# A transformer block on one core: the next token tile is loaded one unit ahead in SyncE's list, and GpSimd issues four of sixteen strip transfers

## The chip, the core and the metric

The kernel runs on one core of a Trainium2 chip. Five engines with an instruction list each work side by side: TensorE (PE in the profile; PEld is its weight load), VectorE (DVE), ScalarE (ACT), GpSimd (POOL) and SyncE (SP), which only issues transfers. They wait for each other through semaphores. The metric is the time of one execution in microseconds (us), median of several.

## The reference

For `x` of 8 x 1024 tokens x 256: `xn = layernorm(x)`, and the output is `x + attention(xn) + ffn(xn)`.

```
qkv = einsum('bse,ehd->bshd', xn, w_qkv);  q, k, v = split(qkv, 3)      # 16 heads of 64
probs = softmax(where(causal, q.k / sqrt(64), neg))
attention = einsum('bshd,hde->bse', einsum('bhqk,bkhd->bqhd', probs, v), w_out)

scores = softmax(xn @ wg); top 2 of 8 experts, their scores made to sum to 1
ffn = sum over the two chosen experts of gate * (relu(row @ w1[e] + b1[e]) @ w2[e] + b2[e])
      # at most 2048 rows an expert; rows beyond that are dropped
```

## The kernel before, in words

Three stages: layernorm, router and routing (up to about 100 us), the eight experts (to about 900 us), and attention with the final sum (from about 910 us to the end). The change lies in the last one, `attention_and_sum`.

**Units and steps.** Attention runs in 64 units: 8 batch entries x 8 pairs of heads. A unit `n` has 20 steps. Each engine has its own list, written out by loops over `(n, s)`, and an engine works its list strictly in order. Rows of the score matrix (tiles of 128 queries, `i` = 0 to 7) are treated in five rounds (steps 0, 4, 8, 12, 16): rows 3 and 2, rows 4 and 1, rows 5 and 0, row 6, row 7. For a round TensorE makes the scores `S` (L1230); VectorE masks them, takes the row minimum of their negative and writes `pr` (L1353); ScalarE exponentiates and sums (L1291); VectorE inverts the sums (`rinv`, L1359); GpSimd scales `pr` by them (L1433).

**Turning the probabilities.** The product with the values needs them transposed (`pT`). Rows 0 to 3 are transposed by TensorE (L1186) and copied by ScalarE (L1281). Rows 4 to 7 are transposed in 32x32 squares by VectorE (L1395, tile `squares`), and then sixteen SBUF-to-SBUF transfers a group put the squares in place: `place(n, 2)` for rows 4 and 5 (96 KB each), `place(n, 3)` for rows 6 and 7 (128 KB each), both L1084. `place(n, 2)` is issued late in unit n (it waits for the squares of row 5, step 14); `place(n - 1, 3)` is issued in unit n, since row 7 of unit n - 1 is squared at step 2 of unit n. TensorE multiplies by the values (L1261, tile `O`) for unit n - 1 in three runs: at step 3 of unit n (rows 0 to 3), at step 7 (rows 4, 5) and at step 15 (rows 6, 7). ScalarE and VectorE split the result into two parts (`oh` L1322, `ol` L1402), TensorE multiplies by `w_out` (L1175, pieces `o0` to `o3`), and VectorE adds to `res` (L1379).

**The next batch entry.** Queries, keys and values are products of the layernorm output `xn`, held transposed. While a batch entry is worked on, the tiles of the next one are brought in, one a unit: SP loads a tile of 128 tokens into `xnt` (L1102), TensorE transposes it at step 1 (piece `xn`, L1164), ScalarE and VectorE split it (L1297, L1369). Nine tiles are there at the start (`AHEAD`), so units 0 to 54 have this piece and units 55 to 63 do not. There is one buffer `xnt`: its next load waits until the transposes of the tile before are done.

**SyncE's list in a unit** is: load `xnt`; load the weights of unit n + 2 (L1072, waits for GpSimd's split of those of n + 1, L1445); `place(n - 1, 3)`; `place(n, 2)`; in even units, the value weights (L1076). Once in eight units it also stores `res` (L1088) and refills it (L1093). A wait at the head of this list holds all that is behind it.

**GpSimd's list in a unit**: scale round 4 of the unit before; split weights (L1438, L1442, L1445); scale round 0 (step 4); `total` (step 5: adds the expert output to one tile of `res`, L1490); `choose` (L1460); scale round 1 (step 8); two gathers `fetch0` and `fetch1` of expert rows (L1468); scale round 2 (step 12); `weigh` and `add` (L1474, L1479); scale round 3. In unit n, `total` adds to tile (n - 1) mod 8 of `res`, and VectorE's addition `o{g}` in unit n waits for it where that tile lies in group g. So `o0`, at VectorE's step 6, waits for GpSimd's `total` in units with n mod 8 of 1 or 2.

Of the kernel before, what the change touches and what calls it, by code (L numbers as in the profile page):

```python
# [19 lines left out]
TILES = TOKENS // P  # L20
# [469 lines left out]
class Start:  # L490


    TILES = QT + 1
# [352 lines left out]
def attention_and_sum(nc, k, x, xn_dram, w_qkv, w_out, pick, y_dram, out, start):  # L846
# [8 lines left out]
    AHEAD = Start.TILES  # L855
    VW = 4 * HDIM
    BL = 32
    QUARTERS = P // BL
# [50 lines left out]
    RUN_OF = {g: j for j, groups in enumerate(RUN_GROUPS) for g in groups}  # L909
# [6 lines left out]
                return n - later, j  # L916
        return None

    POOL_AT = {"split_w": 1, "total": 5, "choose": 6, "fetch0": 8, "fetch1": 9, "weigh": 13, "add": 14, "split_wv": 17}

    turns_of = lambda i: [t for t in TURNS if i in [at[0] for at in TURNS[t]]]
    turn_unit = lambda n, t: n if t in STEP_OF else END_STEP[TURNS[t][0][0]][0]
# [21 lines left out]
    with ExitStack() as c:  # L944
        sb = lambda n, s, d=F32: c.enter_context(nc.sbuf_tensor(n, s, d))
        ps = lambda n, s: c.enter_context(nc.psum_tensor(n, s, F32))
        sem = lambda n: c.enter_context(nc.semaphore(n))
# [16 lines left out]
        xnt = sb("xnt", [P, MODEL])  # L964
# [14 lines left out]
        xnv = xn_dram.rearrange("(t p) m -> t p m", p=P)  # L979
# [51 lines left out]
        score, negmax, expd, scaled = (Count(sem(f"s_{n}"), len(ORDER)) for n in ("score", "negmax", "expd", "scaled"))  # L1031
        recip = Count(sem("s_recip"), len(ROUNDS))
        squared = Count(sem("s_squared"), 2 * len(SQUARED))
        placed = {g: Count(sem(f"s_placed{g}"), 16 * QUARTERS * QUARTERS) for g in (2, 3)}
        pv = Count(sem("s_pv"), RUNS)
        ohi, olo = Count(sem("s_ohi"), RUNS), Count(sem("s_olo"), RUNS)
        filled = Pieces(sem("s_filled"), lambda name: True)
# [25 lines left out]
        def strip(g, a, b):  # L1063

            to, of = slice(b * BL, (b + 1) * BL), slice(a * BL, (a + 1) * BL)
            return wide[g][to, a].rearrange("p x r -> p (x r)"), sq[g][of, b].rearrange("p x k i -> p (x k i)")

        @block.sync
        def _(e):
            def load_w(m):  # L1070
                for c_ in range(MC):
                    e.dma_start(wr[:, 2 * c_:2 * c_ + 2], wv[m % PAIRS][:, c_, :, 0:2 * HDIM]).then_inc(wload.sem, 16)  # L1072

            def load_wv(m):
                for c_ in range(MC):
                    e.dma_start(wvr[:, c_], wvv[m % (PAIRS // 2)][:, c_, :, 2 * HDIM:]).then_inc(wvload.sem, 16)  # L1076

            def place(n, g):
                e.wait_ge(squared.sem, squared.at(n, 4 * g - 4))
                if n > 0:  # L1080
                    e.wait_ge(pv.sem, pv.at(n - 1, RUN_OF[g] + 1))
                for a in range(QUARTERS):
                    for b in range(QUARTERS):
                        e.dma_start(*strip(g, a, b)).then_inc(placed[g].sem, 16)  # L1084

            def store(b, g):
                e.wait_ge(dve.sem, dve.at((b + 1) * PAIRS, f"o{g}"))
                e.dma_start(outv[:, b, 2 * g:2 * g + 2], res[:, 2 * g:2 * g + 2]).then_inc(stored[g].sem, 16)  # L1088

            def refill(b, g):  # L1090
                if b > 0:
                    e.wait_ge(stored[g].sem, stored[g].at(b - 1, 16))
                e.dma_start(res[:, 2 * g:2 * g + 2], xv[:, b, 2 * g:2 * g + 2]).then_inc(rload[g].sem, 16)  # L1093

            load_w(1)
            load_wv(1)
            for n in range(UNITS):
                b, u = n // PAIRS, n % PAIRS
                if n + AHEAD < TILES:
                    if n > 0:  # L1100
                        e.wait_ge(filled.sem, filled.at(n - 1, "xn"))
                    e.dma_start(xnt[:], xnv[n + AHEAD]).then_inc(xload.sem, 16)  # L1102
                if n == 0:
                    e.wait_ge(s_wolo, 1)
                    for g in range(GROUPS):
                        refill(0, g)
                if n + 2 < UNITS:
                    e.wait_ge(wlo.sem, wlo.at(n, MC))
                    load_w(n + 2)
                if n > 0:  # L1110
                    place(n - 1, 3)
                if b > 0 and u == 0:
                    for g in range(3):
                        store(b - 1, g)
                    for g in range(3):
                        refill(b, g)
                if n < UNITS - 1:
                    place(n, 2)
                if n % 2 == 0 and n // 2 + 2 < UNITS // 2:
                    e.wait_ge(wvlo.sem, wvlo.at(n // 2, MC))  # L1120
                    load_wv(n // 2 + 2)
                if b > 0 and u == 0:
                    store(b - 1, 3)
                    refill(b, 3)
            for g in range(GROUPS):
                store(BATCH - 1, g)
            for g in range(GROUPS):
                e.wait_ge(stored[g].sem, stored[g].at(BATCH - 1, 16))

        @block.tensor  # L1130
        def _(e):
# [103 lines left out]
            def values(n, j):  # L1235
                groups = RUN_GROUPS[j]
                if in_squares(n, 2 * groups[0]):
                    g = groups[0]
                    e.wait_ge(placed[g].sem, placed[g].at(n + 1, 0))
                else:  # L1240
                    for m, name in [(turn_unit(n, t), t) for g in groups for i in (2 * g, 2 * g + 1) for t in turns_of(i)]:
                        if by_act(name):
                            e.wait_ge(act.sem, act.at(m, name))
                        else:
                            e.wait_ge(dve.sem, dve.at(m, name))
                if j == 0:
                    e.wait_ge(act.sem, act.at(n // 2 * 2 - 1, "v1"))
                    if n > 0:
                        e.wait_ge(olo.sem, olo.at(n - 1, RUNS))
                else:  # L1250
                    e.wait_ge(act.sem, act.at(n // 2 * 2, "v1"))
                    e.wait_ge(olo.sem, olo.at(n, j))
                for g in groups:
                    KT, o0 = 2 * g + 2, g % 2 * GQ
                    for kt in range(KT):
                        a = P if kt == KT - 1 else 0
                        for h in range(2):
                            hs = slice(h * HDIM, (h + 1) * HDIM)
                            vs = slice(n % 2 * P + h * HDIM, n % 2 * P + (h + 1) * HDIM)
                            turned_p = wide_of(g, h, kt, a // P) if in_squares(n, 2 * g) else pT[g][:, h, kt, a:GQ]  # L1260
                            ins = e.matmul(O[hs, o0 + a:o0 + GQ], vv[n // 2 % 2][:, kt, vs], turned_p,  # L1261
                                           start=(kt == 0), stop=(kt == KT - 1))
                ins.then_inc(pv.sem, 1)
# [73 lines left out]
        def _(e):  # L1337
# [52 lines left out]
            def square(n, i, h):  # L1390
                g, KT = i // 2, i + 1
                if n > 0 and i % 2 == 0 and h == 0:
                    e.wait_ge(placed[g].sem, placed[g].at(n, 0))
                e.wait_ge(scaled.sem, scaled.at(n, SCALE_ORDER.index((i, h)) + 1))
                e.transpose(sq[g][:, :, 2 * h + i % 2, 0:KT, :],  # L1395
                            room_of(n, i, h)[:, OFFSET[i]:OFFSET[i] + KT * P].rearrange("p (k b i) -> p b k i", b=QUARTERS, i=BL)
                            ).then_inc(squared.sem, 1)
# [30 lines left out]
        def _(e):  # L1428
# [18 lines left out]
            def split_wv(m):  # L1447
# [6 lines left out]
                for c_ in range(MC):  # L1454
                    e.tensor_tensor(wvl[:, c_], flat(wvr[:, c_]), wvh[:, c_].bitcast(F32), ALU.subtract).then_inc(wvlo.sem, 1)

            def choose(m):
                if m > 0:
                    e.wait_ge(summed.sem, summed.at(m - 1, 1))
                e.tensor_copy(sel[:], pick[:, m, :]).then_inc(picked.sem, 1)  # L1460
# [33 lines left out]
            for n, s in ALL + END:  # L1494
                r, x = s // SUB, s % SUB
                m, q = back(n, s, SUB)[0], (r - 1) % len(ROUNDS)
                if x == 0 and 0 <= m < UNITS:
                    for j in range(FIRST[q], FIRST[q + 1]):
                        scale(m, j)
                for name, at in POOL_AT.items():  # L1500
                    if s != at:
                        continue
                    if name == "total" and n > 0:
                        total(n - 1)
                    if n == UNITS:
                        continue
                    if name == "choose":
                        choose(n)
                    elif name == "split_w" and n + 1 < UNITS:
                        split_w(n)  # L1510
                    elif name == "split_wv" and n % 2 == 0 and n // 2 + 1 < UNITS // 2:
                        split_wv(n // 2)
                    elif name[:5] == "fetch":
                        fetch(n, int(name[5]))
                    elif name == "weigh":
                        weigh(n)
                    elif name == "add":
                        add(n)
# [38 lines left out]
```

## Time and profile before

| | |
|---|---|
| median of 3 runs | 3215.53 us (3213.91 to 3217.07) |
| profiled execution, its own time | 3221.27 us |
| its span | 3219.3 us |
| PE busy | 2905.2 us, 90% |
| DVE, ACT, POOL busy | 65%, 53%, 46% |
| mean granted TensorE clock | 0.946 of full speed |

Busy shares are averages over three stages with different limits, so each stage has to be looked at alone. "Idle before" a group of instructions is the time in which their engine had nothing running right before them, and the arrow names what ended it. SPq is SyncE's list of transfers: its times are those of the issues, not of the movement of data. A row of several instructions (xN) has the start of the first, and the time to the end of the last for those that touch.

### The profile page before, as it was taken

The page shows a single profiled execution, that of the slowest core. Times are in us where ns is not written, and L with a number is a line of the kernel's source. Part 1 is how long each engine was busy: PE and PEld are TensorE (multiplying, and loading weights), DVE is VectorE, ACT ScalarE, POOL GpSimd, SP SyncE. Part 2 cuts the span into 40 slices and gives each one's busy share as a digit, 9 for nine tenths or more (in the row PEclk, how much of TensorE's full clock was granted, in tenths as well). Part 3 has the DMA queues.
Part 4 walks back from the last instruction along what each step waited for, and adds up shares of the span by engine and source line. Part 5 has one row for each costly group of instructions (what it writes and reads, how often), then busy time and mean ns, then how long its engine had stood idle before and what let it go on. Part 6 is the DMA issues. An engine that isn't in the chain of part 4 may idle for free.

```text
span 3219.3 us, 61016 instructions
## 1 busy us (share of the span) xinstructions
PE 2905.2 (90%) x21321; PEld 2337.3 (73%) x21321; DVE 2107.3 (65%) x4448; ACT 1714.3 (53%) x3934; POOL 1465.3 (46%) x2127
## 2 busy tenths in 40 slices
PE   4699999999989988999899898989889998999998
PEld 3589998999967666777667676766667766777776
DVE  7744434444357776777777777777767777778785
ACT  3444444454445555555555555555555555556664
POOL 3122222122135555555555555555555555556663
PEclk8799999999999998999899999999989999999999
DMA  7112222122135455546555555555565455555653
GB/s 236 49 47 73 74 72 71 55 67 74 52 99 122 117 128 147 132 116 148 126 133 123 138 129 126 131 142 123 125 152 125 118 123 148 129 128 149 150 126 91
DMA packets 252805, 371.57 MB, mean 115 GB/s; under 512 B 77392, under 2 KB 177744, under 8 KB 252512
## 3 DMA queue, kind: packets, MB, share of 16 engines
q1 hardware_dynamic: 240192, 334.14, 40.9%
q0 software_dynamic: 12320, 33.60, 3.6%
q8 instruction: 174, 2.85, 0.4%
q14 instruction: 119, 0.97, 0.1%
HBM read 102.80 MB, written 33.55 MB: 42 GB/s over the span
## 4 chain that ended last, share of the span: by engine, by line
PE 36%; SPq 15%; DVE 7%; issue 5%; DMA 5%; POOL 3%; ACT 1%; DVEq 0%; POOLq 0%; ACTq 0%
SPq L1084 14%; PE O L1261 13%; PE S L1230 9%; DMA xnt<-xn 4%; PE W L1175 4%; PE W L1186 4%; DVE squares L1395 3%; PE W L1141 3%; PE W L1156 3%; DVE pr L1353 2%; POOL pr L1433 2%; PE W L1164 1%; SPq L1076 1%; ACT pr L1291 1%; DMA out<-res 1%
## 5 line engine op out<-in xcount | busy, mean ns | idle before, releaser
L1433 POOL TENSOR_SCALAR pr<-pr,rinv 128x512 f32<-128x512 f32 (+7 forms) x1024 | 747.8, 746 | 959.8 <-DVE rinv L1359 958.6
L1291 ACT ACTIVATE pr<-pr,negm 128x512 f32<-128x512 f32 (+7 forms) x1024 | 784.4, 771 | 146.4 <-DVE negm L1353 146.2
L1353 DVE CUSTOM_DVE_ANT_0 pr<-S,late 128x512 f32<-128x512 f32 (+7 forms) x1024 | 718.1, 752 | 154.8 <-PE S L1230 154.4
L1261 PE MATMUL O<-pT,vv 128*64 128x256 f32 (+1 forms) x5120 | 631.4, 405 | 1.8 <-DMA pT<-squares 1.1
L1261 PEld LDWEIGHTS O<-pT,vv 128*64 128x64 f32 x5120 | 398.7, 155 | 222.8 <-issue 82.0
L1395 DVE STREAM_TRANSPOSE squares<-pr 128x640 f32<-128x640 f32 x504 | 494.8, 1020 | 0.3 <-POOL pr L1433 0.3
L832 DVE TENSOR_TENSOR hl<-h,hh 128x512 fp32r<-128x512 f32 x256 | 190.6, 745 | 322.0 <-ACT hh L793 311.0
L789 ACT ACTIVATE h<-pH,b1c 128x512 f32<-128x512 f32 x256 | 175.8, 687 | 369.8 <-PE pH L719 342.0
L1281 ACT ACTIVATE pT<-W 128x512 f32<-128x512 f32 (+3 forms) x520 | 200.2, 435 | 321.0 <-PE W L1186 320.3
L731 PE MATMUL pY<-w2h,hh 128*128 128x256 f32 x1024 | 287.8, 281 | 2.5 <-DVE hl L832 2.5
L731 PE MATMUL pY<-w2l,hh 128*128 128x256 f32 x1024 | 289.0, 282 | 0.0
L731 PE MATMUL pY<-w2h,hl 128*128 128x256 f32 x1024 | 287.8, 281 | 0.0
L1402 DVE TENSOR_TENSOR ol<-O,oh 128x256 fp32r<-128x256 f32 (+1 forms) x192 | 98.2, 512 | 235.5 <-ACT oh L1322 235.5
L1230 PE MATMUL S<-khf,qh 64*128 64x512 f32 (+2 forms) x1024 | 220.5, 426 | 1.5 <-DVE negm L1353 1.5
L1141 PE MATMUL W<-xnh,wh 128*128 128x512 f32 x512 | 215.2, 420 | 2.7 <-DVE klf L1387 1.5
L1186 PE MATMUL W<-ident,pr 128*128 128x128 f32 x1332 | 201.8, 282 | 17.0 <-POOL pr L1433 11.9
L1164 PE MATMUL W<-ident,xnt 128*128 128x128 f32 x110 | 31.5, 383 | 204.9 <-DMA xnt<-xn 204.9
L719 PE MATMUL pH<-xh,w1h 128*128 128x512 f32 x512 | 206.4, 403 | 4.6 <-DVE xl L804 2.6
L719 PE MATMUL pH<-xl,w1h 128*128 128x512 f32 x512 | 202.7, 396 | 0.0
L1141 PE MATMUL W<-xnh,wl 128*128 128x512 f32 x512 | 202.7, 396 | 0.0
L719 PE MATMUL pH<-xh,w1l 128*128 128x512 f32 x512 | 202.6, 396 | 0.0
L1141 PE MATMUL W<-xnl,wh 128*128 128x512 f32 x512 | 202.6, 396 | 0.0
(175 smaller groups left out, 6346.5 us busy)
## 6 DMA issues: line engine op xcount, KB each, us to landing
pT<-squares SPq DMA_DIRECT2D x1008, 128.0 KB
pT<-squares SPq DMA_DIRECT2D x1008, 96.0 KB, 2.1
y<-yb SPq DMA_DIRECT2D x128, 128.0 KB, 1.7
wr<-in_L_attn_w_qkv SPq DMA_DIRECT2D x128, 128.0 KB, 2.3
x<-in_L_attn_x SPq DMA_DIRECT2D x16, 512.0 KB, 9.0
xn<-xn SPq DMA_DIRECT2D x16, 512.0 KB, 4.7
w1r<-in_L_ffn_w SPq DMA_DIRECT2D x8, 1024.0 KB
w2r<-in_L_ffn_w SPq DMA_DIRECT2D x8, 1024.0 KB
```

The source lines that it names most:

```text
L719: ins = e.matmul(pH[hc % 4][:], w[par][:, m, ws], xx[q][:, m, :], start=(n == 0), stop=(n == 3 * MC - 1))
L731: ins = e.matmul(pY[t % 2][:], hs[q][:, hc, ts_], ws[par][:, hc, :], start=(hc == 0 and n == 0), stop=(hc == HC - 1 and n == 2))
L1084: e.dma_start(*strip(g, a, b)).then_inc(placed[g].sem, 16)
L1141: ins = e.matmul(W, ws[:, 2 * m + of_k], xs[:, t0:t0 + HT, m, :], start=(i == 0), stop=(i == 3 * MC - 1))
L1186: ins = e.transpose(W[:, at * P:(at + 1) * P], room_of(unit, i, h)[:, cols], k["ident"][:])
L1230: ins = e.matmul(S[h][:, off + f * HALF:off + f * HALF + cols], t[hs, i * P:(i + 1) * P], u[f][n % 2][hs, 0:cols], start=(j == 0), stop=(j ...
L1261: ins = e.matmul(O[hs, o0 + a:o0 + GQ], vv[n // 2 % 2][:, kt, vs], turned_p, start=(kt == 0), stop=(kt == KT - 1))
L1281: ins = e.activation(dst, src, ACT.Copy) if by_act(name) else e.tensor_copy(dst, src)
L1291: e.activation(p, p, ACT.Exp, bias=negm[:, c0:c0 + 1], scale=-1.0, accum_out=rsum[:, c0:c0 + 1]).then_inc(expd.sem, 1)
L1353: e.tensor_tensor_reduce(room_of(n, i, h)[:, off:off + w], S[h][:, off:off + w], late[:, SEQ - w:], 1.0, -MASKED, ALU.add, ALU.min, negm[: ...
L1395: e.transpose(sq[g][:, :, 2 * h + i % 2, 0:KT, :], room_of(n, i, h)[:, OFFSET[i]:OFFSET[i] + KT * P].rearrange("p (k b i) -> p b k i", b=Q ...
L1433: e.tensor_scalar(p, p, rinv[:, c0:c0 + 1], 1.0, ALU.mult, ALU.mult).then_inc(scaled.sem, 1)
```

## The change

In SyncE's list the load of `xnt` stands behind the weight load of the same unit and is that of the next unit's tile; the first one stands ahead of the loop. It waits for the transposes of this unit's tile (`filled.at(n, "xn")`). Of the sixteen transfers of `place(n - 1, 3)`, SyncE issues twelve; GpSimd issues the last four, at its step 4, after the scaling of round 0 and ahead of `total`. They count on a semaphore of their own, `pool_placed`, for which TensorE (before the third run) and VectorE (before it writes the squares of row 6 again) wait as well.

```diff
-    POOL_AT = {"split_w": 1, "total": 5, "choose": 6, "fetch0": 8, ...
+    POOL_AT = {"split_w": 1, "place3": 4, "total": 5, "choose": 6, "fetch0": 8, ...
@@
-        placed = {g: Count(sem(f"s_placed{g}"), 16 * QUARTERS * QUARTERS) for g in (2, 3)}
+        placed = {2: Count(sem("s_placed2"), 16 * QUARTERS * QUARTERS), 3: Count(sem("s_placed3"), 16 * QUARTERS * (QUARTERS - 1))}
+        pool_placed = Count(sem("s_pool_placed"), 16 * QUARTERS)
@@ def place(n, g):
-                for a in range(QUARTERS):
+                for a in range(QUARTERS - (g == 3)):
@@ sync
+            e.dma_start(xnt[:], xnv[AHEAD]).then_inc(xload.sem, 16)
             load_w(1)
             load_wv(1)
             for n in range(UNITS):
                 b, u = n // PAIRS, n % PAIRS
-                if n + AHEAD < TILES:
-                    if n > 0:
-                        e.wait_ge(filled.sem, filled.at(n - 1, "xn"))
-                    e.dma_start(xnt[:], xnv[n + AHEAD]).then_inc(xload.sem, 16)
@@
                 if n + 2 < UNITS:
                     e.wait_ge(wlo.sem, wlo.at(n, MC))
                     load_w(n + 2)
+                if n + 1 + AHEAD < TILES:
+                    e.wait_ge(filled.sem, filled.at(n, "xn"))
+                    e.dma_start(xnt[:], xnv[n + 1 + AHEAD]).then_inc(xload.sem, 16)
                 if n > 0:
                     place(n - 1, 3)
@@ tensor, values(n, j); vector, square(n, i, h) alike
                     e.wait_ge(placed[g].sem, placed[g].at(n + 1, 0))
+                    if g == 3:
+                        e.wait_ge(pool_placed.sem, pool_placed.at(n + 1, 0))
@@ gpsimd
+            def place_rest(n):
+                e.wait_ge(squared.sem, squared.at(n + 1, 0))
+                if n > 0:
+                    e.wait_ge(pv.sem, pv.at(n - 1, RUN_OF[3] + 1))
+                for b in range(QUARTERS):
+                    e.dma_start(*strip(3, QUARTERS - 1, b)).then_inc(pool_placed.sem, 16)
@@
+                    if name == "place3" and n > 0:
+                        place_rest(n - 1)
```

SyncE's list through a unit (2 here; every later one is alike), as it was. `pT<-squares` of 32x1024 is `place(n - 1, 3)`, that of 32x768 is `place(n, 2)`; lines are one higher in the changed kernel:

```order
L1102 DMA xnt<-xn 128x256 [waits s_filled]
L1072 DMA wr<-in_L_attn_w_qkv 128x2x128 [waits s_wlo_a]
L1072 DMA wr<-in_L_attn_w_qkv 128x2x128
L1084 DMA pT<-squares 32x1024 [waits s_pv,s_squared]
L1084 DMA pT<-squares 32x1024 x15
L1084 DMA pT<-squares 32x768 [waits s_pv,s_squared]
L1084 DMA pT<-squares 32x768 x15
```

And the same unit as it stands now:

```order
L1073 DMA wr<-in_L_attn_w_qkv 128x2x128 [waits s_wlo_a]
L1073 DMA wr<-in_L_attn_w_qkv 128x2x128
L1110 DMA xnt<-xn 128x256 [waits s_filled]
L1085 DMA pT<-squares 32x1024 [waits s_pv,s_squared]
L1085 DMA pT<-squares 32x1024 x11
L1085 DMA pT<-squares 32x768 [waits s_pv,s_squared]
L1085 DMA pT<-squares 32x768 x15
```

The load of the tile that a unit transposes has moved from right behind `place(n - 1, 2)` of the unit before to ahead of both placements of the unit before.

GpSimd's list from the end of the weight split to the gathers, as it was:

```order
L1445 TENSOR_TENSOR wl<-wr,wh 128x256
L1433 TENSOR_SCALAR pr<-pr,rinv 128x512 [waits s_recip] x2
L1433 TENSOR_SCALAR pr<-pr,rinv 128x384 [waits s_recip] x2
L1490 TENSOR_TENSOR res<-res,yg 128x256 [waits s_dve,s_sum1]
L1460 COPY sel<-pick 128x4 [waits s_summed]
L1433 TENSOR_SCALAR pr<-pr,rinv 128x640 [waits s_recip] x2
L1433 TENSOR_SCALAR pr<-pr,rinv 128x256 [waits s_recip] x2
L1468 DMA yg<-y,sel 128x256 [waits s_picked] x2
```

And now:

```order
L1450 TENSOR_TENSOR wl<-wr,wh 128x256
L1438 TENSOR_SCALAR pr<-pr,rinv 128x512 [waits s_recip] x2
L1438 TENSOR_SCALAR pr<-pr,rinv 128x384 [waits s_recip] x2
L1467 DMA pT<-squares 32x1024 [waits s_pv,s_squared]
L1467 DMA pT<-squares 32x1024 x3
L1502 TENSOR_TENSOR res<-res,yg 128x256 [waits s_dve,s_sum1]
L1472 COPY sel<-pick 128x4 [waits s_summed]
L1438 TENSOR_SCALAR pr<-pr,rinv 128x640 [waits s_recip] x2
L1438 TENSOR_SCALAR pr<-pr,rinv 128x256 [waits s_recip] x2
L1480 DMA yg<-y,sel 128x256 [waits s_picked] x2
```

The four issues stand between the scaling of round 0 and `total` (the addition to `res`); the scaling of round 1 and all behind it follow them.

## Rows read from the trace of the kernel before

**Rows 1.** Tile `xnt`: durations in ns (min/median/max), idle before it, landing.

```profile
L1164 PE MATMUL W<-ident,xnt x110: 271/421/449, 925.5 to 2879.8; 128*128 128x128 f32 x110
L1102 SPq DMA_DIRECT2D xnt<-xn x55: 467/505/663, 912.5 to 2877.3; - x55
  DMA xnt<-xn: 204.9, 54
DMA to landing us min/median/max: 2.1/2.4/2.9
```

**Rows 2.** SyncE's queue through a unit (start us, us, what, count).

```profile
2007.41 0.89 SPq L1072 DMA_DIRECT2D wr<-in_L_attn_w_qkv  x2
2008.40 30.15 SPq L1084 DMA_DIRECT2D pT<-squares  x32
2038.59 1.19 SPq L1076 DMA_DIRECT2D wvr<-in_L_attn_w_qkv  x2
2039.82 0.50 SPq L1102 DMA_DIRECT2D xnt<-xn  x1
```

**Rows 3.** Stretches: us, busy of each engine, granted clock, DMA share, GB/s.

```profile
962.90:2884.00 1921.10, 1722.24 (x13040) 1321.26 (x13036) 1390.36 (x3021) 1063.07 (x2650) 1050.83 (x1590) 0.93 0.54 130
2889.85:3142.90 253.05, 243.55 (x1954) 189.26 (x1954) 204.74 (x448) 157.90 (x393) 158.99 (x240) 1.00 0.57 143
3004.40:3035.90 31.50, 30.45 (x247) 23.62 (x246) 25.64 (x57) 19.72 (x50) 20.96 (x32) 1.00 0.54 129
```

**Rows 4.** TensorE's timeline at the piece `xn` and the next transposes.

```profile
925.53 0.38 PE L1164 MATMUL W<-ident,xnt 128*128 128x128 f32 x2
958.41 0.66 PE L1164 MATMUL W<-ident,xnt 128*128 128x128 f32 x2 [6.76 <-DMA xnt<-xn]
...
993.27 0.41 PE L1164 MATMUL W<-ident,xnt 128*128 128x128 f32 x2 [2.76 <-DMA xnt<-xn]
...
997.62 1.09 PE L1186 MATMUL W<-ident,pr 128*128 128x128 f32 x8
...
2879.62 0.52 PE L1164 MATMUL W<-ident,xnt 128*128 128x128 f32 x2 [2.51 <-DMA xnt<-xn]
...
2885.52 0.66 PE L1186 MATMUL W<-ident,pr 128*128 128x128 f32 x4
```

**Rows 5.** Waits from 2915 to 3142 us: total, times, longest.

```profile
PE W L1186 <- POOL pr L1433: 8.1, 8, 1.0
PE O L1261 <- DMA pT<-squares: 1.1, 1, 1.1
```

**Rows 6.** Timeline of unit 58: GpSimd.

```profile
3011.58 2.48 POOL L1433 TENSOR_SCALAR pr<-pr,rinv 128x512 f32<-128x512 f32 x4
3014.03 0.73 POOL L1490 TENSOR_TENSOR res<-res,yg 128x256 f32<-128x256 f32 x1
3014.83 0.18 POOL L1460 COPY sel<-pick 128x4 uint32<-128x4 uint32 x1
3017.27 2.49 POOL L1433 TENSOR_SCALAR pr<-pr,rinv 128x640 f32<-128x640 f32 x4 [2.25 <-DVE rinv L1359]
3019.90 1.03 POOL L1468 DMA_INDIRECT yg<-y,sel  x1
3021.24 0.96 POOL L1468 DMA_INDIRECT yg<-y,sel  x1 [0.30 <-issue]
3023.34 2.49 POOL L1433 TENSOR_SCALAR pr<-pr,rinv 128x128 f32<-128x128 f32 x4 [1.14 <-DVE rinv L1359]
```

**Rows 7.** Timeline of unit 58: VectorE and TensorE.

```profile
3014.87 0.69 DVE L1379 TENSOR_TENSOR res<-W,res 128x512 f32<-128x512 f32 x1 [0.64 <-POOL res L1490]
3016.99 0.18 DVE L1359 RECIPROCAL rinv<-rsum 128x4 f32<-128x4 f32 x1 [1.43 <-ACT pr L1291]
3017.42 0.42 DVE L1402 TENSOR_TENSOR ol<-O,oh 128x256 fp32r<-128x256 f32 x1 [0.25 <-ACT oh L1322]
3019.12 0.36 PE L1175 MATMUL W<-woh,oh 128*128 128x256 f32 x1
3021.49 1.56 DVE L1395 STREAM_TRANSPOSE squares<-pr 128x640 f32<-128x640 f32 x2
3027.25 1.83 DVE L1395 STREAM_TRANSPOSE squares<-pr 128x768 f32<-128x768 f32 x2
```

**Rows 8.** GpSimd's and SyncE's issues: ns min/median/max, first and last start.

```profile
L668 POOL DMA_INDIRECT xg<-xn,slot_token x8: 942/946/2535, 136.2 to 147.5; - x8
L1084 SPq DMA_DIRECT2D pT<-squares x2016: 507/592/2192, 944.1 to 3179.7; - x184
```

More of the change, by code:

```diff
@@ L917, in run_at @@
         return None
-    POOL_AT = {"split_w": 1, "total": 5, "choose": 6, "fetch0": 8, "fetch1": 9, "weigh": 13, "add": 14, "split_wv": 17}
+    POOL_AT = {"split_w": 1, "place3": 4, "total": 5, "choose": 6, "fetch0": 8, "fetch1": 9, "weigh": 13, "add": 14, "split_wv": 17}
     turns_of = lambda i: [t for t in TURNS if i in [at[0] for at in TURNS[t]]]
@@ L1393, in square @@
                     e.wait_ge(placed[g].sem, placed[g].at(n, 0))
+                    if g == 3:
+                        e.wait_ge(pool_placed.sem, pool_placed.at(n, 0))
                 e.wait_ge(scaled.sem, scaled.at(n, SCALE_ORDER.index((i, h)) + 1))
@@ L1506, in _ @@
                         continue
-                    if name == "choose":
+                    if name == "place3" and n > 0:
+                        place_rest(n - 1)
+                    elif name == "choose":
                         choose(n)
```

## The prediction

> **What bounds the kernel now.** I read the page's split by slices and then the waits of the attention stage, which is 2300 of 3219 us. TensorE has one large wait there: 204.9 us in 54 places in front of the transposes of `xnt`, ended by that tile's transfer [rows 1]. Nothing else holds TensorE for more than a microsecond or two. SyncE's queue says why the tile is late: its issue (2039.82) stands directly behind a run of 32 strip issues and the value weights [rows 2]. The second half of that run cannot start before row 5 is squared, late in the unit; the tile then lands 2.4 us after its issue [rows 1]. TensorE wants it at step 1 of the next unit, and so a chain goes round once a unit: squares, sixteen issues, load, transposes, scores, squares.
>
> The profile holds its own counter-example. The units from 55 on have no `xnt` load but the same strips, products and softmax. The table of stretches shows both kinds [rows 3]. With the load: a granted clock of 0.93, near but not at the upper of TensorE's two levels (2.4 GHz), and units that take (2879.62 - 958.41) / 53 = 36.25 us [rows 4]. Without it: clock 1.00, TensorE busy 243.55 of 253.05 us, and units of 31.50 us, in which it is busy 30.45 [rows 3]. The loss is thus larger than the wait of 3.7 us. From the transposes of `xnt` to the next ones (L1186) TensorE took 4.35 us at 993.27, but 5.90 us at 2879.62 [rows 4], and most units look like the second: the wait is followed by a stretch at the lower level (1.2 GHz), which costs 1.5 us.
>
> **The load.** It moves ahead of both placements. It now waits for this unit's transposes (step 1), which come before the squares of row 7 (step 2) that the placement behind it wants; so this wait holds nobody, and the tile has nearly a unit to land. The 0.5 us issue in front of twelve strips instead of sixteen still ends them sooner than before. I take the wait as gone, all of it.
>
> What is late next stands in the last units too: TensorE waits 1.0 us for GpSimd's scaling of round 0, in each of 8 units [rows 5], since GpSimd splits weights right before it. A unit with an `xn` piece adds its transposes on TensorE, 0.41 us [rows 4], and one subtraction on VectorE just ahead of the reciprocal for which GpSimd waits, of about the same size. The first fits into the 1.0 us, the second pushes GpSimd by most of its length. I take 0.35 us, hence 31.85 us a unit. (Bounds: 31.5 if all hides, 31.9 if none does: -19 to +3 us over the kernel.)
>
> - 53 intervals of 36.25 - 31.85 = 4.40: 233.2 us.
> - The interval from 925.53 to 958.41 holds a wait of 6.76 us [rows 4]; unit 0 has less work, and I take back 1.0 for the next limit: 5.8 us.
> - The slow stretch behind the last transposes, 5.90 - 4.35: 1.5 us.
> - The wait of 1.1 us for strips [rows 5], in the unit where a store had held SyncE: four strips fewer take at least 4 x 0.51 us [rows 8], so it goes: 1.1 us.
>
> Sum 241.6 us. 3221.3 - 241.6 = 2979.7 us by the profiled execution.
>
> **The four issues on GpSimd.** SyncE gets 4 x 0.59 us a unit back [rows 8], worth nothing now that it has slack. GpSimd pays. The trace has no plain transfer issued by GpSimd, so p, the distance from one issue to the next, is bounded: from below by SyncE's 0.6 us (0.59 median, [rows 8]); from above by the longest gather issue, 2.54 us plus the 0.30 us gap between two [rows 6, 8]: 2.84 us. The nearest row is the pair of gathers: 3019.90 to 3021.24 is 1.34 us, and the shortest gather is 0.94, with the gap 1.24 [rows 6, 8]. I take p = 1.25, since a strip has 32 rows where a gather has 128, but no row shows that rows count.
>
> Three things stand behind them, read in unit 58.
>
> - `total` (3014.03) starts 4p later. In units with n mod 8 of 1 or 2, VectorE's `o0` waits for it: this happens here already (0.64 us, [rows 7]). `o0` would start at 3014.87 + 4p; behind it on VectorE come the reciprocal and `ol`, so `ol` ends 0.69 + 0.18 + 0.42 + 0.1 later, at 3016.3 + 4p. TensorE wants it at 3019.12 for `o1` [rows 7]. TensorE is late by 4p - 2.8, for p = 1.25: 2.2 us. Nothing later in the unit gives it back, as TensorE has no other idle time but the 1.0 us whose chain moves with it. These are 16 units: 35 us. A stop of 1.1 us left the clock at 1.00 in the stretch that holds it [rows 3, 5], while one of 2.51 was followed by the slow level [rows 4]. 2.2 lies between; I charge a third of 1.5 us: 8 us.
> - The scaling of round 1 can start at 3015.1 + 4p instead of 3017.27 and has row 4 ready for the squares (3021.49) by 3016.0 + 4p for its first head [rows 6, 7]: in time up to p = 1.37. Nothing for the other units.
> - The gathers and the scaling of round 2 follow: it would start near 3020.2 + 4p = 3025.2 instead of 3023.34 and have row 5's first head ready 1.6 us later, 3026.8, before VectorE's 3027.25 [rows 6, 7]. Nothing, but only just.
>
> For larger p VectorE falls behind in every unit, by 4p - 5.45 at row 5's squares. It has about 1.95 us of idle time behind them before the last round's reciprocal, on which GpSimd's scaling and then TensorE's transposes hang. A general unit is late by 4p - 7.4, from p = 1.85 on.
>
> **Where a page bears on it.** The two gather issues beside a busy VectorE in unit 58 took 1.03 and 0.96 us [rows 6]. The Trainium skill (SBUF — State Buffer, section "SBUF: two separate sides") says that a transfer issued by GpSimd has its descriptors written by GpSimd's cores, which are locked out of a shared port while VectorE runs an instruction in a two-port mode, and gives 620 ns for such a transfer alone and about 3100 ns beside a VectorE copy. By the first figure the sum would be near the lower bound below, by the second it would be the slower rival. VectorE's work in that stretch is of other kinds (one operand in PSUM), and the trace's gathers side with the short figure.
>
> **The sum.** 2979.7 + 35 + 8 = 3022.7 us for the profiled execution, which is 5.7 us above the median of the runs shown (3221.27 against 3215.53). Expected median: 3017 us.
>
> **The rivals.**
>
> 1. *GpSimd's issues are cheap*, p up to 0.7: 4p - 2.8 is 0, nothing is late. 2979.7 - 5.7 = 2974 us. For it: a strip is simpler than a gather. Against it: no GpSimd issue in the trace is under 0.94 us.
> 2. *They are dear enough to reach every unit*, p = 2: 16 x (5.2 + 1.5) + 48 x 0.6 = 136 us, giving 3110 us. For it: one issue of 2.54 us; four in a row are not shown. Against it: 946 ns is the median of such issues.
> 3. *Slower than before.* The same place, GpSimd's step 4: the loss 16 x (4p - 1.3) + 48 x (4p - 7.4) eats the 241.6 us at p = 2.41. At p = 2.84, the upper bound, it is 161 + 190 = 351 us: 3325 us. It decides at 2.41 us an issue.
> 4. *The clock stays at 0.93* though TensorE waits less: 54 units x 7% of 31.85 are 120 us less gain, some 3137 us. Against it: 1.00 over 253 us of the same work, and 0.93 only beside the waits [rows 3].
> 5. *The load isn't the chain*: its transfer is still late, or the wait turns up at the next strips. Within 0.2% of before, 3215 us. Against it: the last units place the same strips without a wait, but the one of 1.1 us.
>
> **How the numbers follow.** Forecast (p from 1.0 to 1.5) 0.58; rival 1, 0.2; rival 2, 0.12; rival 3, 0.04; rival 4, 0.04; rival 5, 0.02. The range takes in p = 0.7 and, below it, half of the 19 us that a unit of 31.5 would give: 2966. Above, p = 1.65 gives 16 x (3.8 + 1.5) = 85 us, 3059; with a little of rival 2, 3064. Faster by more than 0.2% (about what this kernel's measurement can tell from no change): all but rivals 3 and 5, 0.94; within 0.2%, 0.02; slower, 0.04.
>
> **What would show it.** The wait of TensorE for `xnt` (204.9 us) is gone, and `xnt`'s issue stands some 25 us ahead of its transposes. The granted clock from 963 us on is near 1.00. TensorE waits about 1 us a unit for GpSimd at L1438. The distance of two strip issues on GpSimd is 1.25 us. In 16 units, and only there, VectorE's addition `o0` waits for GpSimd's `total`, 4 to 5 us, and TensorE waits some 2 us for `ol`. I am wrong if units without that wait take much over 31.9 us, if the wait for `xnt` has become one for strips, or if the issues on GpSimd take under 0.7 or over 1.5 us.

## The result: 2980 us, 7.3% faster, near the lower bound of the term on GpSimd

| | before | changed |
|---|---|---|
| median | 3216.3 us (4 runs, 3213.9 to 3218.9) | 2980.22 us (4 runs, 2979.75 to 2982.94) |
| ratio | | 0.9268, 95% interval 0.9252 to 0.9284 |
| span of the profiled execution | 3219.3 us | 2978.6 us |

The forecast was 3017 us, with a range of 2966 to 3064. The direction, the mechanism and the size of the gain from the load came out as forecast; the loss charged to GpSimd's four issues (43 us) did not appear. The nearest case was rival 1, cheap issues, 2974 us.

**The wait for the load.** The changed kernel's answer for tile `xnt` (durations in ns, first and last start):

```profile
L1165 PE MATMUL W<-ident,xnt x110: 270/271/273, 922.9 to 2639.8; 128*128 128x128 f32 x110
L1110 SPq DMA_DIRECT2D xnt<-xn x54: 461/466/535, 928.9 to 2612.9; - x54
```

There is no waiting row under it any more, where [rows 1] has 204.9 us in 54 places. The transposes themselves have gone from a median of 421 ns to 271: they are no longer run right after a stop. The last load is issued at 2612.9 and wanted at 2639.8, 27 us later.

From these rows and [rows 1] the whole gain can be counted. First to last transposes: 1954.3 us before, 1716.9 now, 237.4 us less. What stands ahead of the first ones: 2.6 us less. What stands behind the last ones: 339.5 against 338.8 us. Sum 240.7 us, the difference of the spans.

**The clock.** Stretches of the changed kernel: us, busy of PE, PEld, DVE, ACT, POOL, granted clock, DMA share, GB/s. The first is units with an `xn` piece, the second units without.

```profile
963.00:2640.00 1677.00, 1612.10 (x12916) 1253.34 (x12914) 1360.74 (x2992) 1048.61 (x2626) 1153.28 (x1780) 1.00 0.58 148
2655.00:2900.00 245.00, 236.08 (x1888) 183.02 (x1888) 199.81 (x437) 152.19 (x377) 169.37 (x262) 1.00 0.54 142
```

Against 0.93 in [rows 3] the clock is 1.00, and TensorE is busy 96% of both. Per unit it was busy 1722.24 us / 53.0 = 32.5 us before (1921.10 / 36.25 units) and is now busy 1612.10 / 52.6 = 30.7 us (1677 / 31.9 units) with the same work: 1.8 of the 4.35 us by which a unit got shorter (36.25 to 31.90 on average, without the first) go with the clock.

**What is left.** The waits of the changed kernel from 950 to 2900 us: total, times, longest.

```profile
PEld W L1187 <- DVE xnl L1372: 68.7, 53, 1.3
PE W L1187 <- POOL pr L1438: 68.0, 62, 1.2
DVE res L1382 <- POOL res L1502: 44.2, 16, 3.1
PE O L1264 <- DMA pT<-squares: 5.0, 6, 1.8
```

The second row is the wait of [rows 5], now in every unit. The first is the same stop as TensorE's weight loads show it. The name in it is only that of the last thing that ended before: in the unit at 2102 us `xnl` was over 1.0 us before the load began (2101.97 against 2102.95), so it did not end the wait, though it can delay what did (see e7 below). The third row is the expected one: VectorE waits for GpSimd's `total` in 16 units. TensorE shows no wait behind it.

**GpSimd in such a unit**, to be read beside [rows 6], and below VectorE and TensorE, beside [rows 7]:

```profile
2770.80 2.48 POOL L1438 TENSOR_SCALAR pr<-pr,rinv 128x512 f32<-128x512 f32 x4
2773.22 2.08 POOL L1467 DMA_DIRECT2D pT<-squares  x4
2775.32 0.74 POOL L1502 TENSOR_TENSOR res<-res,yg 128x256 f32<-128x256 f32 x1
2776.13 0.18 POOL L1472 COPY sel<-pick 128x4 uint32<-128x4 uint32 x1
2777.05 2.50 POOL L1438 TENSOR_SCALAR pr<-pr,rinv 128x640 f32<-128x640 f32 x4 [0.73 <-DVE rinv L1362]
2779.70 1.06 POOL L1480 DMA_INDIRECT yg<-y,sel  x1 [0.16 <-issue]
```

All of GpSimd's strip issues (ns, min/median/max):

```profile
L1467 POOL DMA_DIRECT2D pT<-squares x252: 489/512/606, 955.4 to 2932.2; - x126
```

VectorE and TensorE in the same unit:

```profile
2776.17 0.69 DVE L1382 TENSOR_TENSOR res<-W,res 128x512 f32<-128x512 f32 x1 [2.72 <-POOL res L1502]
2776.78 0.17 DVE L1362 RECIPROCAL rinv<-rsum 128x4 f32<-128x4 f32 x1
2778.34 0.36 PE L1176 MATMUL W<-woh,oh 128*128 128x256 f32 x1
```

Four issues take 2.08 us with no gap: p = 0.52 us, less than half of the 1.25 that I took, and below SyncE's 0.59. So a plain strip of 32 rows is much cheaper to issue than a gather of 128, which still takes 1.06 us in the same unit. The scaling of round 1 even waits 0.73 us for its reciprocal. VectorE's `o0` is over (2776.8) 1.5 us before TensorE comes to `o1` (2778.34).

### The profile page after: what moved, and what is told of

It is laid out like the page before. It is cut to its first block, busy times and chain, and to the rows that moved or that the text cites. A ratio compares the mean times of both kernels' runs of the same rounds, so it can differ in the third digit from the quotient of the medians.

```text
span 2978.6 us, 61141 instructions
## 1 busy us (share of the span) xinstructions
PE 2802.8 (94%) x21321; PEld 2276.4 (76%) x21321; DVE 2089.6 (70%) x4448; ACT 1710.1 (57%) x3934; POOL 1601.7 (54%) x2379
## 4 chain that ended last, share of the span: by engine, by line
POOL 24%; PE 23%; issue 17%; ACT 3%; DVE 2%; DMA 0%; POOLq 0%; DVEq 0%; ACTq 0%
POOL pr L1438 14%; PE O L1264 5%; PE S L1231 5%; PE W L1187 4%; PE W L1142 3%; PE W L1176 3%; POOL wl L1450 3%; PE W L1157 2%; ACT pr L1294 2%; POOL wh L1447 2%; POOL wvl L1460 1%; POOL yg L1486 1%; POOL wr L1443 1%; POOL wvh L1457 1%; DVE squares L1400 1%
## 5 line engine op out<-in xcount | busy, mean ns | idle before, releaser
L1264 PE MATMUL O<-pT,vv 128*64 128x256 f32 (+1 forms) x5120 | 542.0, 362 | 5.0 <-DMA pT<-squares 5.0
L1264 PEld LDWEIGHTS O<-pT,vv 128*64 128x64 f32 x5120 | 346.7, 137 | 184.4 <-issue 20.1
L1187 PE MATMUL W<-ident,pr 128*128 128x128 f32 x1332 | 211.2, 283 | 79.2 <-POOL pr L1438 71.8
L1187 PEld LDWEIGHTS W<-ident,pr 128*128 128x128 f32 x1332 | 146.4, 141 | 145.5 <-DVE xnl L1372 68.7
L1382 DVE TENSOR_TENSOR res<-W,res 128x512 f32<-128x512 f32 x256 | 175.6, 686 | 57.9 <-POOL res L1502 44.2
```

The source lines that it names most:

```text
L1187: ins = e.transpose(W[:, at * P:(at + 1) * P], room_of(unit, i, h)[:, cols], k["ident"][:])
```

## The experiments

Twelve kernels; every ratio is to the kernel before, on the same chip.

| run | median, us | ratio (95%) |
|---|---|---|
| e1_load_only | 2980.5 | 0.9272 (0.9256 to 0.9287) |
| e2_strips_only | 3215.2 | 0.9998 (0.9989 to 1.0008) |
| e3_eight_on_gpsimd | 2982.7 | 0.9274 (0.9259 to 0.9290) |
| e4_eight_after_total | 2975.5 | 0.9240 (0.9226 to 0.9254) |
| e5_twelve_on_gpsimd | 3020.4 | 0.9378 (0.9364 to 0.9393) |
| e6_load_after_12 | 2979.9 | 0.9264 (0.9249 to 0.9280) |
| e7_split_behind_reciprocal | 2961.3 | 0.9201 (0.9189 to 0.9214) |
| e8_scale_first | 2981.0 | 0.9261 (0.9248 to 0.9273) |
| e9_squares_behind_ol | 2967.9 | 0.9225 (0.9213 to 0.9238) |
| e10_squares_split | 3294.3 | 1.0225 (1.0208 to 1.0241) |
| e11_both_small | 2958.9 | 0.9195 (0.9183 to 0.9208) |
| e12_strips_before_scale | 2958.7 | 0.9192 (0.9180 to 0.9205) |

### One part at a time

**The load alone** (the kernel before, with the load moved as in the change; all sixteen strips on SyncE).

> The load stands ahead, SyncE issues all sixteen strips, GpSimd none. Theory A (the load is the change; GpSimd's four issues only shorten the strips in the one unit in eight in which a store holds SyncE): TensorE's wait for xnt is 0, units of 31.8 to 31.9 us, and in the 8 units with n mod 8 = 1 the strips are late by 4 x 0.64 = 2.6 us more than in the changed kernel; about 2980 + 18 = 2998 us. Rival B (the strips on GpSimd are what lets the load's gain through): strips are late in every unit, over 3050 us. Rival C (GpSimd's issues cost something): 2975 us or less.

2980.5 us: the same as the changed kernel. Rivals B and C fall, and so does the 18 us that theory A gave the strips. In this kernel TensorE waits 6.0 us in 10 places for strips, in the changed one 5.0 in 6. So taking four issues off SyncE does not end those waits. A row from the changed kernel (its columns as in [rows 3]), inside a unit with n mod 8 = 1, points elsewhere:

```profile
1980.00:1985.00 5.00, 5.00 (x38) 4.58 (x38) 4.55 (x13) 4.45 (x12) 4.07 (x7) 1.00 1.06 242
```

The DMA share is 1.06: the engines that move the data are full, where refills of `res`, gathers and strips come together. The wait in that unit (1.79 us, to 1990.28) lasted although the last of SyncE's twelve issues was out at 1985.4. The trace's landing events, which the views above do not list, show what ended it: the last of SyncE's twelve strips landed at 1990.24, 5.4 us after its issue began, and GpSimd's four had landed before (their last recorded event is at 1982.1; 56 of 64 are recorded). All six waits of the changed kernel are of this kind, with GpSimd's last recorded landing 6 us or more ahead. From SyncE's first issue to TensorE's start these units took 13.1 to 14.1 us with twelve issues, and with sixteen (this run) 13.1 to 14.9. With only eight on SyncE (e3 and e4 below) the waits are all but gone.

**The strips alone** (the changed kernel, with the load at its old place).

> GpSimd issues the four strips, the load stands at its old place behind place(n-1, 2). Theory A: the chain squares, sixteen strips of rows 4 and 5, load, transposes is as long as before, so TensorE waits some 3.7 us a unit for xnt and the granted clock is 0.93 to 0.95: 3210 to 3218 us. Rival B (fewer issues in SyncE's list shorten the chain, 4 x 0.64 us a unit): about 3216 - 55 x 2.6 = 3073 us.

3215.2 us, no change (0.9998), and the wait of [rows 1] is back:

```profile
PE W L1165 <- DMA xnt<-xn: 206.2, 54, 8.1
```

Theory A holds. Moving four issues off SyncE shortens `place(n - 1, 3)`, which has slack, and not `place(n, 2)`, behind which the load stood.

**How early is early enough?** Four strips on GpSimd, and the load inside `place(n, 2)`:

```diff
-                    place(n, 2)
+                    place(n, 2, range(QUARTERS)[:3])
+                    if n + 1 + AHEAD < TILES:
+                        e.wait_ge(filled.sem, filled.at(n, "xn"))
+                        e.dma_start(xnt[:], xnv[n + 1 + AHEAD]).then_inc(xload.sem, 16)
+                    place(n, 2, range(QUARTERS)[3:])
```

> Four strips on GpSimd; the load stands behind twelve of the sixteen strips of place(n, 2), four issues (2.55 us) earlier than before. Theory A (a long wait also costs 1.5 us a unit at the lower clock, a short one doesn't): the chain is 36.25 - 2.55 - 1.5 = 32.2 us, TensorE waits about 1 us for xnt, granted clock near 1.00: about 2980 + 54 x 0.35 = 3000 us. Rival B (any wait is followed by the slow stretch): 33.7 us a unit, clock 0.95, 3080 us.

2979.9 us: four issues earlier give the whole gain. TensorE waits for the tile 7.1 us in 16 places only, where theory A had some 54 us in all:

```profile
PE W L1188 <- POOL pr L1439: 45.2, 61, 1.2
PE W L1166 <- DMA xnt<-xn: 7.1, 16, 2.4
```

A unit takes 31.85 us, so theory A's 32.2 were 0.35 us too long; rival B (33.7 us a unit, 3080 us) is out by 100 us. 2.55 us of issue time took away 4.40 us a unit. The other 1.85 us agree with the 1.8 us that went with the clock above (it is 1.00 here too): the slow stretch behind each stop was itself part of the chain that led to the next late load.

### The price of GpSimd's issues

Eight strips instead of four, then twelve, at the same place (`a in range(QUARTERS - 2, QUARTERS)` and `- 3`):

> Eight strips instead of four on GpSimd, ahead of total. Theory A (TensorE is late by k x p - 2.8 us in the units with n mod 8 of 1 or 2, k issues of p = 0.52 us): 8 x 0.52 - 2.8 = 1.4 us in 16 units, 22 us, with no clock loss as the stop is short, and the 5 us of waits for strips go: 2980 + 22 - 5 = 2997 us; VectorE's o0 waits 4.8 us in 16 units. Rival B (the issues are free at any number, the slack was misjudged): 2975 us. Rival C (GpSimd becomes late in every unit): 3030 us or more.

> Twelve strips on GpSimd ahead of total. Theory A (late by 12 x 0.52 - 2.8 = 3.4 us in 16 units, and a stop this long is followed by a stretch at the lower clock, 1.5 us): 55 us without, 79 us with the clock, less 5 us of strip waits: 3030 to 3054 us. The other 48 units gain and lose nothing (they are late from 7.4 us of issues on, here 6.2). Rival B (every unit late by 2 us or more): over 3100 us.

2982.7 and 3020.4 us. The waits of VectorE for `total`, then of TensorE for VectorE, are the key. For eight strips:

```profile
PE W L1176 <- DVE res L1382: 4.8, 16, 0.6
DVE res L1382 <- POOL res L1503: 70.1, 15, 4.8
```

and for twelve:

```profile
PE W L1176 <- DVE res L1382: 36.5, 16, 3.6
DVE res L1382 <- POOL res L1503: 108.7, 18, 8.0
DVE squares L1400 <- POOL pr L1438: 31.1, 87, 1.4
```

TensorE is late by 0 us for four strips, 0.3 for eight, 2.3 for twelve, each in 16 units. My formula, the number of issues times p, less 2.8, gives 1.4 and 3.4 for the last two. Its slope is right and its slack too small: TensorE's `o1` does not need the `ol` behind `o0` on VectorE. By the code it needs the `ol` of the first run (`RUN_OF[1]` is 0), long done, and the PSUM bank that `o0` used, which is free as soon as the addition `o0` has ended. The wait is indeed put down to `DVE res`. That end stands 0.6 us behind `o0`'s start (in the unit above, 2776.17 to 2776.78, where the next instruction starts) and not 1.4, so the slack is 3014.87 + 0.60 against 3019.12 [rows 7]: 3.65 us. With it, 8 issues (4.01 us in the trace) give 0.4 and 12 give 2.4.

The run with twelve also shows what such stops do to the clock. Here are two of them with the stretch behind each:

```profile
2790.46 0.39 PE L1176 MATMUL W<-woh,oh 128*128 128x256 f32 x1 [2.21 <-DVE res L1382]
2824.39 0.58 PE L1176 MATMUL W<-woh,oh 128*128 128x256 f32 x1 [2.17 <-DVE res L1382]
```

```profile
2788.00:2796.00 8.00, 5.79 (x43) 4.99 (x43) 5.98 (x16) 4.51 (x12) 6.69 (x12) 1.00 0.71 191
2824.00:2832.00 8.00, 7.61 (x44) 6.75 (x45) 6.57 (x18) 3.90 (x10) 6.66 (x10) 0.79 0.43 98
```

After 2.21 us of idle time the clock stays at 1.00, and after 2.17 us it falls for a while. Of the 15 stops of 2.17 to 2.23 us in this trace six have a stretch at the lower level with them, and the one of 3.64 us has one too. So the third of 1.5 us that I charged for a stop of 2.2 us was a fair price; with four issues it was not due because the stop itself did not come. (The profiled execution, 3029.4 us, is the longest of the four; the others have 3016.8 to 3022.2 us at a slightly higher mean clock.) The last row of the run with twelve is the other threshold, the general one: VectorE waits for the scaling in front of squares, 0.36 us on average. TensorE isn't late by it: the other units still take 31.8 us, as expected up to 7.4 us of issues.

**The same eight, behind `total`** (`"total": 5, "choose": 6, "place3": 7`):

> Eight strips on GpSimd as in the run before with eight, but issued behind total and choose. Theory A (GpSimd's issues cost TensorE time only through total, for which VectorE's o0 waits): the wait of VectorE for total is as before the change (about 1 us in all), nothing is late, the waits for strips are gone: 2974 to 2980 us. Rival B (it is the scaling of round 1 and of round 2 behind the issues that costs): the same time as with eight ahead of total.

2975.5 us. VectorE's wait for `total` is down from 70.1 to 10.8 us and that for the scaling of round 1 comes to 2.2 us in all. Theory A holds: only what stands ahead of `total` costs. TensorE's waits for strips have shrunk from 5.0 us to 0.7 us, which about accounts for the 4.7 us to the changed kernel; the intervals of the two ratios overlap, so the gain itself is not proven.

### What bounds the changed kernel

```diff
-    DVE_STEP = {"xn": 3, ...
+    DVE_STEP = {"xn": 4, ...
```

> The changed kernel, and VectorE's xnl subtraction one step later, behind the reciprocal and ol of round 0. Theory A (the 0.35 us by which a unit with xn is longer than one without is VectorE's subtraction ahead of the reciprocal for which GpSimd waits): units with xn take 31.5 to 31.55 us; 2980 - 55 x 0.35 = 2961 us. Rival B (it is TensorE's own transposes): 2980 us.

2961.3 us against 2961, and clear of the changed kernel. That it agrees to the microsecond is luck: the five executions run from 2958.5 to 2963.6 us. Its VectorE at the start of a unit:

```profile
2118.30 0.13 DVE L1362 RECIPROCAL rinv<-rsum 128x4 f32<-128x4 f32 x1
2118.35 0.66 DVE L1407 TENSOR_TENSOR ol<-O,oh 128x512 fp32r<-128x512 f32 x1
2118.93 0.41 DVE L1372 TENSOR_TENSOR xnl<-W,xnh 128x256 fp32r<-128x256 f32 x1
```

The subtraction stands behind the reciprocal now. Thus the 0.35 us a unit was this 0.4 us instruction on VectorE, not TensorE's transposes. TensorE's wait is shorter, and goes by another name:

```profile
PE W L1187 <- DVE xnl L1372: 41.8, 53, 0.8
```

```profile
2118.54 2.48 POOL L1438 TENSOR_SCALAR pr<-pr,rinv 128x512 f32<-128x512 f32 x4
2119.37 1.30 PE L1187 MATMUL W<-ident,pr 128*128 128x128 f32 x8 [0.78 <-DVE xnl L1372]
```

I read it as still the wait for GpSimd's scaling. TensorE starts 0.83 us after the scaling does (2119.37 and 2118.54), as in the changed kernel (2102.99 and 2102.15, 0.84 us); `xnl` now happens to end in between, at 2119.34.

**Taking this wait away** (on top of e7). GpSimd scales round 0 first (`"total": 4, "choose": 4, "split_w": 4, "place3": 8`), VectorE squares row 7 behind the reciprocal, SyncE places rows 6 and 7 ahead of the weight load:

> As the run before, and what stands ahead of GpSimd's scaling of round 0 moved behind it: GpSimd scales round 0, then total and choose, then splits weights, then scales round 1, then issues the four strips; VectorE squares row 7 behind the reciprocal of round 0; SyncE places rows 6 and 7 ahead of the weight load. Theory A (TensorE's 1.0 to 1.1 us a unit of waiting for the scaling is the only thing that the units still lose): 30.5 to 30.8 us a unit, 2961 - 63 x 0.8 = 2910 us. Rival B (the next limit is as near: the squares of row 7 come 0.7 us later and the strips or VectorE take over): 2950 us or more.

2981.0 us: theory A falls. The wait for the scaling is gone, and another has come instead (this kernel's waits, then its VectorE and TensorE in a unit):

```profile
PE W L1176 <- DVE xnl L1372: 55.9, 54, 1.0
```

```profile
2104.99 2.34 DVE L1400 STREAM_TRANSPOSE squares<-pr 128x1024 f32<-128x1024 f32 x2
2107.25 0.65 DVE L1407 TENSOR_TENSOR ol<-O,oh 128x512 fp32r<-128x512 f32 x1
2107.82 0.41 DVE L1372 TENSOR_TENSOR xnl<-W,xnh 128x256 fp32r<-128x256 f32 x1
2108.34 0.36 PE L1176 MATMUL W<-woh,oh 128*128 128x256 f32 x1 [1.04 <-DVE xnl L1372]
```

The squares, moved out of the reciprocal's way, stand in the way of `ol` and `xnl`, which `o0` needs. I then put them behind those (in step 4, ahead of the minima):

> As e8, but VectorE's squares of row 7 stand behind ol and xnl instead of ahead of them (step 4, still ahead of the minima of round 1). In e8 TensorE's wait for the scaling was gone and one of 1.04 us in front of o0 had come in its place, ended by xnl, which stood behind 2.34 us of squares. Theory A (that order is all of it): o0's wait falls to 0.3 us or less, and the minima of round 1, 0.5 us later than in e8, cost 0 to 0.3 us at the scores of round 2: 2981 - 63 x 0.7 = 2937 us, 2930 to 2945. Rival B (VectorE is the limit in this stretch, and the wait moves on to the minima): 2955 us or more.

2967.9 us: 13 us better than e8, but not 2937. The wait for `xnl` is gone and two small ones have come, 0.35 us for the minima in each unit and 33 waits for strips that land late (by the landing events GpSimd's four end 27 of them, among them those put down to "issue"):

```profile
PE S L1231 <- DVE negm L1356: 18.9, 54, 0.4
PE O L1264 <- issue: 14.0, 23, 1.9
PE O L1264 <- DMA pT<-squares: 13.7, 10, 2.9
```

**The second head's squares later still** (step 6):

> As e9, but only the first head of row 7 is squared at step 4, the second at step 6 behind the addition o0, so that the minima of round 1 come 1.2 us earlier than in e9. Theory A (strips have room): no wait for the minima, 0 to 0.3 us a unit less than e9, 2920 to 2937 us. Rival B (the strips of rows 6 and 7 now land later than step 15 wants them, by 0.5 to 1 us a unit): 2950 to 2980 us, and the wait is ended by the strips' transfers.

3294.3 us, slower than the kernel before. Rival B was right in kind and far too mild in size. TensorE waits for strips in every unit, and the clock falls again (0.93 in the second row):

```profile
PE O L1264 <- DMA pT<-squares: 225.7, 53, 5.6
```

```profile
963.00:2900.00 1937.00, 1709.00 (x12883) 1293.76 (x12883) 1355.63 (x2984) 1043.95 (x2619) 1152.54 (x1783) 0.93 0.54 129
```

The chain of this kernel through one unit (start, us, what) shows it:

```profile
2088.42 1.16 DVE squares L1400
2089.60 0.51 SPq L1085
...
2096.30 1.05 SPq L1085
2097.39 5.88 DMA pT<-squares
2103.32 5.15 PE O L1264 x32
```

And its stretches, granted clock and DMA share:

```profile
2090.00:2095.00 5.00, 5.00 (x41) 4.58 (x38) 4.53 (x12) 4.23 (x12) 4.70 (x9) 1.00 0.77 189
2095.00:2100.00 5.00, 3.78 (x25) 2.68 (x23) 4.37 (x8) 1.85 (x5) 4.07 (x6) 1.00 1.04 229
2103.00:2108.50 5.50, 5.18 (x34) 3.08 (x34) 0.00 (x0) 0.00 (x0) 5.33 (x9) 0.69 0.75 252
```

The last strip needs 5.88 us from issue to landing, and the landing events say that it is SyncE's (2103.27). The 2.1 us that the profile's page gives are those of the 96 KB strips. For SyncE's last strip of 128 KB the landing events give, as the median of the units, 2.4 us in the kernel before, 3.9 in the changed one (not all its events are recorded) and 5.5 here. The DMA engines are at 1.04 here, where SyncE's strips run beside GpSimd's, the gathers and the weight load. Squares that come late don't just shift the strips, they move them into a crowd. And the 4.5 us stop is followed by a clock of 0.69 and `O` in 5.15 us instead of the 3.46 us of the kernel with the load alone.

**Away from the gathers** (e9, with `"place3": 7`, ahead of the scaling of round 1):

> As e9, but GpSimd's four strips are issued ahead of its scaling of round 1 instead of behind it, 2.5 us earlier and away from the two gathers. Theory A (e9 lost 20 us in 24 waits for strips because the last four were issued late, among the gathers): 2968 - 20 = 2948 us. Rival B (SyncE's twelve end those waits, or the transfers of that stretch saturate the DMA engines): 2962 to 2970 us.

2958.7 us: half of what theory A expected. TensorE still waits 29.9 us in 42 places for strips. It is 9 us better than e9, so GpSimd's four were part of it. The other part is SyncE's twelve: in all 42 places they land last, GpSimd's four at least 2.2 us before TensorE starts, and their last issue was out 3.0 to 5.3 us before. Whether those landings would come sooner with fewer transfers under way was not tested.

**The two small gains together** (e7, and eight strips behind `total`):

> The changed kernel with two of the variants together: VectorE's xnl behind ol (19 us less in its own run), and eight strips on GpSimd behind total and choose (4.7 us less in its own run). Theory A (they act on separate waits, the reciprocal and the late strips of one unit in eight): 2961.3 - 4.7 = 2956.6 us. Rival B (the second's gain was within the noise of its run, or the earlier reciprocal makes the eight issues late for the scaling of round 1): 2961 us or more.

2958.9 us, 2.4 us less than e7 alone and within its interval. It and e12 beat both kernels; the sure part is that of e7.

## Why the prediction was right, and where its terms were off

- **What bounds the kernel.** Right. The load alone gives the whole change, the strips alone give none.
- **The load's sum, 241.6 us.** Right within 1 us, by 240.7, and this close by luck, since its terms miss by 1 to 3 us and cancel. The 53 full units were forecast at 31.85 us and take 31.90: 2.9 us less gain. The first interval gained 6.9 us instead of 5.8. What stands ahead of the first transposes gained 2.6 us, which the sum did not have. What stands behind the last ones gained 0.7 us instead of 2.6: of the 1.1 us of the strips' wait half is left (0.52 us at 2754.73 in this very unit), as the issues did not end it (e1).
- **The clock.** Right: 1.00 from the first units on; rival 4 is out. e6 bears out that the slow stretch was part of the chain.
- **The next limit.** Right: GpSimd's scaling, 1.0 to 1.1 us a unit. The 0.35 us for the `xn` piece was put on VectorE's subtraction, which e7 confirmed.
- **GpSimd's four issues, 43 us.** Wrong in size. The mechanism is there: `o0` waits for `total` in 16 units, 2.8 us each (forecast: 4 to 5), and nowhere else; but it never reached TensorE. Two numbers were off. The price p was taken from the nearest row, a gather, as 1.25 us and measured 0.52; the lower bound from SyncE's issues was the better guide. The slack was taken as 2.8 us, since I let `o1` wait for VectorE's `ol` behind `o0`; it is 3.65 us, as e3 and e5 measured. With p = 0.52 either slack gives 0, and the forecast would have been 2974 us. The 6 us to the result are the 5.7 that were taken off because the profiled execution of the kernel before was above its median; that of the changed kernel (2980.38) is at its median.
- **Rival 3's break-even at 2.41 us an issue** was never tested; twelve issues, 6.2 us in all, cost 40 us.
- **The range's lower end** was given as 2966; 2974 less half of 19 us is 2964.5.
- **The two figures of the Trainium skill** (SBUF — State Buffer, section "SBUF: two separate sides"), 620 and 3100 ns for a transfer issued by GpSimd. They are times of a transfer; what the trace has is the time that GpSimd takes to issue one: 489 to 606 ns, with VectorE busy 81% of the time. Nothing like the long one shows beside this kernel's VectorE work (which is not all with an operand in PSUM, as the prediction has it: the squares go from `pr` to `squares`, both outside it).

## What to carry to other kernels

A transfer that nobody needs for long, put behind a run of issues that must wait for this iteration's last product, ties the next iteration's start to this one's end. The place in the queue counts, not the number of issues: taking four issues away elsewhere gave nothing, moving the load past four gave everything. And where the last iterations lack the suspected piece, they are a measurement of the kernel without it: here they gave 31.5 us and the new bottleneck, and with an estimated 0.35 us for the missing piece the new time of a unit within 0.05 us. A wait is put down to what ended last before it, which need not be what it waited for: compare the distance to the suspect in two kernels, as with `xnl` above. For an operation that the trace does not have, keep both bounds; a dearer relative with more work in it isn't nearer because it is on the same engine.

## What the runs showed of the hardware

- A plain transfer of 32 rows of 4 KB within SBUF takes GpSimd 0.49 to 0.61 us to issue, back to back, against 0.96 to 1.06 us and a 0.30 us gap for a gather of 128 rows of 1 KB in the changed kernel.
- With the DMA share at 1.04, the last 128 KB strip of a run landed 5.9 us after its issue (e10); the median over the units of the kernel before is 2.4 us, at a mean DMA share of 0.54.
- Stops of TensorE of some 1.1 us, one a unit, left the granted clock at 1.00 in all 62 places from 950 to 2900 us of the changed kernel. Of the 15 stops of 2.17 to 2.23 us with twelve issues, six had a stretch at the lower level with them. Of the 54 of 2.45 to 7.7 us before the change, all but one had (2.76 us, [rows 4]), and of the 54 of 3.4 to 5.6 us in e10 all but six.
